# Expert loops over pairs written out; their last turn normalises and transposes tiles 0 and 1 for the stage behind them

## The reference, cut to what matters

```python
x = x + _L0_ffn_ref(_layernorm(x), gate_w, gate_b, expert_w, expert_b)   # 8 experts, the 2 best, relu
x = x + _L1_attn_ref(_layernorm(x), Wq, Wk, Wv, Wo)                      # q * cumsum(k * v), then Wo
x = x + _L1_xattn_ref(_layernorm(x), ctx_2048, ...)
x = x + _L1_ffn_ref(_layernorm(x), W1, Wg, W2, ...)                      # 1 shared and 7 routed experts, silu
x = x + _L2_attn_ref(_layernorm(x), W_qkv, W_o)                          # 16 heads, ALiBi, causal softmax
x = x + _L2_xattn_ref(_layernorm(x), ctx_2048, ...)
```

## Time and profile before

| what | us |
|---|---|
| median of 3 runs | 2199.65 |
| the runs | 2194.30 to 2200.67 |
| the profiled execution, its own time | 2198.75 |
| its span | 2197.0 |
| PE busy | 1883.8 (86%) |
| DVE busy | 1492.2 (68%) |
| ACT busy | 1083.9 (49%) |
| POOL busy | 1083.1 (49%) |
| L0f, from its first gate matmul to its last add | 434.7 to 504.0 |
| L1a, from its first matmul | 508.0 |
| L1f, from its first matmul to its last add | 564.0 to 746.8 |
| L2a, from its first matmul | 751.0 |

### The profile page before, as it was taken

One profiled execution on the slowest core, in us unless ns is written; L12 is line 12 of the kernel. 1 busy time (PEld: TensorE's weight loads), 2 busy tenths in 40 slices (PEclk: granted clock), 3 DMA queues, 4 the chain that ended last, 5 costly groups with the idle time before them and its releaser, 6 DMA issues.

```text
span 2197.0 us, 32570 instructions
## 1 busy us (share of the span) xinstructions
PE 1883.8 (86%) x11446; PEld 1386.8 (63%) x11446; DVE 1492.2 (68%) x2547; ACT 1083.9 (49%) x2348; POOL 1083.1 (49%) x791
## 2 busy tenths in 40 slices
PE   7577788798899896899999999678888789877999
PEld 6111157545789774677777777566777655545888
DVE  5688843474764484777777776489999858665543
ACT  4444422253223264666666666366666546534443
POOL 2599931120880173755555554499999800012221
PEclk9788899599899898999999999789999889998999
DMA  4111002120400010100000001000000020000000
GB/s 158 45 34 34 0 1 75 51 102 3 171 0 0 0 30 20 49 23 1 1 1 1 1 1 39 19 1 1 1 1 27 1 78 1 1 0 1 6 9 8
DMA packets 22162, 54.80 MB, mean 25 GB/s; under 512 B 8463, under 2 KB 13752, under 8 KB 19592
## 3 DMA queue, kind: packets, MB, share of 16 engines
q1 hardware_dynamic: 22024, 53.01, 7.2%
HBM read 44.61 MB, written 1.05 MB: 21 GB/s over the span
## 4 chain that ended last, share of the span: by engine, by line
PE 53%; DVE 17%; POOL 11%; issue 11%; ACT 7%; SPq 1%; DMA 0%; DVEq 0%; POOLq 0%; ACTq 0%
POOL sbuf L1308 4%; PE psum L4121 4%; DVE sbuf L2289 3%; PE psum L4182 3%; PE psum L3499 2%; PE psum L4254 2%; POOL sbuf L1316 2%; DVE psum L3084 1%; PE psum L4607 1%; POOL sbuf L1107 1%; PE psum L4628 1%; PE psum L4614 1%; PE psum L4169 1%; PE psum L4153 1%; PE psum L4125 1%
## 5 line engine op out<-in xcount | busy, mean ns | idle before, releaser
L1308 POOL TENSOR_TENSOR sbuf<-sbuf 128x1035 f32<-128x1035 f32 x128 | 248.3, 1969 | 0.9 <-ACT sbuf L1946 0.9
L4254 PE MATMUL psum<-sbuf 128*128 128x128 f32 (+1 forms) x1024 | 146.4, 295 | 58.9 <-ACT sbuf L1955 41.4
L1955 ACT ACTIVATE sbuf<-sbuf 128x1001 f32<-128x1001 f32 (+1 forms) x128 | 141.5, 1137 | 104.6 <-DVE sbuf L3092 70.6
L4254 PEld LDWEIGHTS psum<-sbuf 128*128 128x128 f32 (+1 forms) x1024 | 128.5, 155 | 80.5 <-ACT sbuf L1955 60.1
L1263 POOL TENSOR_TENSOR sbuf<-sbuf 128x512 f32<-128x512 f32 x64 | 66.7, 1042 | 187.7 <-DVE sbuf L2980 187.7
L1107 POOL TENSOR_TENSOR sbuf<-sbuf 128x1024 f32<-128x1024 f32 x64 | 149.8, 2354 | 17.0 <-DVE sbuf L2289 17.0
L2289 DVE TENSOR_TENSOR_SCAN sbuf<-psum,sbuf 128x1024 f32<-128x1024 f32 x64 | 144.7, 2278 | 12.5 <-ACT psum L1429 6.2
L3447 PE MATMUL psum<-sbuf 96*128 96x512 bf16 x256 | 83.7, 439 | 74.3 <-DVE sbuf L2289 33.0
L1879 ACT ACTIVATE sbuf<-psum,sbuf 128x128 f32<-128x128 f32 x256 | 90.6, 366 | 107.3 <-DVE sbuf L2974 107.3
L3084 DVE SCALAR_TENSOR_TENSOR psum<-sbuf,psum 128x1024 f32<-128x1024 f32 (+1 forms) x96 | 122.3, 1274 | 16.5 <-PE psum L4244 9.4
L1429 ACT ACTIVATE psum<-psum,sbuf 128x1016 f32<-128x1016 f32 x64 | 69.0, 1082 | 125.7 <-PE psum L3447 125.7
(11 more groups left out here) (895 smaller groups left out, 5143.1 us busy)
## 6 DMA issues: line engine op xcount, KB each, us to landing
sbuf<-sbuf SPq DMA_DIRECT2D x42, 128.0 KB, 2.4
sbuf<-w_p_d SPq DMA_DIRECT2D x8, 512.0 KB, 3.8
sbuf<-w_qkv_d SPq DMA_DIRECT2D x3, 768.0 KB, 4.3
sbuf<-w_e_d SPq DMA_DIRECT2D x1, 2048.0 KB, 7.8
sbuf<-w_gu_d SPq DMA_DIRECT2D x1, 2048.0 KB, 10.0
sbuf<-w_gu_d SPq DMA_DIRECT2D x2, 1024.0 KB, 7.9
sbuf<-w_dn_d SPq DMA_DIRECT2D x1, 2048.0 KB, 17.1
sbuf<-w_q_d SPq DMA_DIRECT2D x1, 2048.0 KB, 8.1
```

Of the source, the lines that this page charges most:

```text
L1308: pool.tensor_tensor(P_r[g % 7][:, :, :], rows.unsqueeze(2).to_broadcast([128, 23, 45]), cols.unsqueeze(1).to_broadcast([128, 23, 45]), AL ...
L1955: act.activation(Q_r[g % 6][:, 0:w], Q_r[g % 6][:, 0:w], ACT.Silu, scale=q8_p[n % 2][:, h:h + 1]).then_inc(silu_done, 1)
L4254: last = pe.matmul(Gps[0:m, c, :], Q_r[g % 6][:, 128 * c:128 * c + m], ident[:, :], start=h == 0 and c % 4 == 0, stop=h == 7, skip_group_c ...
```

## The change

Four things are edited.

- The loops of L0f and of L1f become Python loops, so that their four turns are written out with constants as wait values and addresses. L1a keeps its hardware loops.
- In the written-out loops the tiles prepared for the next turn are `(2 * b + 2) % 8` and `(2 * b + 3) % 8`: in the last turn tiles 0 and 1, which the first turn has finished.
- The lead-in of L1a is taken out on all engines; `unT0` and `unT1` come from the last turn of L0f.
- In L2a the statistics, factors, normalisation, transposes and copies of tiles 0 and 1 are taken out; queries, keys and values of these two tiles read `unT0` and `unT1`. The counters of later stages are lowered to match. DVE gets one more wait, ahead of its second bias add, for POOL's centring of the weights, whose scratch memory overlaps `L2a_P[1]`.

```diff
@@ POOL, ACT, DVE, PE: L0f; ACT, DVE, PE: L1f @@
-            with pe.Fori(0, 4) as b:
+            for b in range(4):
@@ DVE, L0f; the same at L2559, L2581, L2585 and in L1f at L2722, L2725, L2790, L2791 @@
-                dve.bn_stats(st0[:, 0:6], x_next[:, 2*b+0, :])
+                dve.bn_stats(st0[:, 0:6], x[:, (2 * b + 2) % 8, :])
@@ ACT, between L0f and L1a @@
-            act.sem_inc(L1a_scalar_done, 4)
-            act.wait_ge(L0f_scalar_done, 74)
-            act.wait_ge(L1a_vector_done, 6)
-            act.activation(st0[:, 8:9], st0[:, 7:8], ACT.Ln, bias=eps5[:, 0:1]).then_inc(L1a_scalar_done, 1)
...
-            act.activation(unT1[:, 0:2, :], ps1[:, 0, 0:256], ACT.Copy).then_inc(L1a_scalar_done, 1)
+            act.sem_inc(L1a_scalar_done, 9)
@@ DVE, between L0f and L1a @@
-            dve.sem_inc(L1a_vector_done, 3)
+            dve.sem_inc(L1a_vector_done, 9)
             dve.wait_ge(L0f_vector_done, 135)
-            dve.bn_stats(st0[:, 0:6], x[:, 0, :]).then_inc(L1a_vector_done, 1)
...
-            dve.tensor_scalar(u1[:, :], x[:, 1, :], st1[:, 6:7], st1[:, 9:10], ALU.subtract, ALU.mult).then_inc(L1a_vector_done, 1)
-            dve.wait_ge(L1a_matmul_done, 2)
@@ PE, between L0f and L1a @@
-            pe.wait_ge(L1a_vector_done, 8)
...
-            last.then_inc(L1a_matmul_done, 1)
+            pe.sem_inc(L1a_matmul_done, 2)
+            pe.wait_ge(L0f_scalar_done, 80)
             pe.wait_ge(L1a_w_loaded, 32)
             pe.wait_ge(L1a_scalar_done, 9)
@@ POOL, L2a @@
-            L2a_norm(0)
-            L2a_norm(1)
             for i in range(8):
@@ ACT, L2a @@
-            L2a_rstd(0, 2, 1)
-            L2a_unTc(0)
-            L2a_rstd(2, 8, 2)
             L2a_qTc(0)
+            L2a_rstd(2, 8, 1)
             L2a_vc(0)
-            L2a_unTc(1)
@@ DVE, L2a @@
                 dve.wait_ge(score_done, L2a_start['score'] + n + 1)
+                if n == 0 and a == 1:
+                    dve.wait_ge(centred_done, L2x_start['centred'] + 8)
...
             dve.wait_ge(L1f_vector_done, 253)
-            L2a_stats(0, 2)
@@ PE, L2a @@
-                pe.wait_ge(unT_done, L2a_start['unT'] + n + 1)
+                un = (unT0, unT1)[n] if n < 2 else L2a_unT
+                if n == 0:
+                    pe.wait_ge(L1f_scalar_done, 109)
+                elif n == 1:
+                    pe.wait_ge(vc_done, L2a_start['vc'] + 1)
+                else:
+                    pe.wait_ge(unT_done, L2a_start['unT'] + n - 1)
...
-            L2a_uTr(0)
             pe.wait_ge(L2a_w_loaded, 32)
             L2a_qk(0)
             L2a_value(0)
-            L2a_uTr(1)
```

More of the change, by code:

```diff
@@ L1583, in _ @@
             act.wait_ge(L0f_scalar_done, 5)
-            with act.Fori(0, 4) as b:
+            for b in range(4):
                 act.wait_ge(L0f_vector_done, 27*b + 31)
@@ L2524, in _ @@
             dve.wait_ge(L0f_scalar_done, 5)
-            with dve.Fori(0, 4) as b:
+            for b in range(4):
                 dve.wait_ge(L0f_matmul_done, 12*b + 3)
@@ L2558, in _ @@
                 dve.tensor_tensor(r0_1[:, :, :], ps1[:, 2, :].rearrange('p (e o) -> p e o', e=2), b_e0[:, 512:1024].rearrange('p (e o) -> p e o', e=2), ALU.add).then_inc(L0f_vector_done, 1)
-                dve.bn_stats(st1[:, 0:6], x_next[:, 2*b+1, :])
+                dve.bn_stats(st1[:, 0:6], x[:, (2 * b + 3) % 8, :])
                 dve.wait_ge(L0f_pool_done, 6*b + 3)
@@ L2718, in _ @@
             dve.wait_ge(L1f_scalar_done, 17)
-            with dve.Fori(0, 4) as b:
+            for b in range(4):
                 dve.wait_ge(L1f_vector_done, 51*b + 1)
                 dve.sem_inc(dve_waited, 1)
-                dve.bn_stats(st0[:, 0:6], x_next[:, 2*b+0, :]).then_inc(L1f_vector_done, 1)
+                dve.bn_stats(st0[:, 0:6], x[:, (2 * b + 2) % 8, :]).then_inc(L1f_vector_done, 1)
                 dve.wait_ge(L1f_vector_done, 51*b + 2)
                 dve.sem_inc(dve_waited, 1)
-                dve.bn_stats(st1[:, 0:6], x_next[:, 2*b+1, :]).then_inc(L1f_vector_done, 1)
+                dve.bn_stats(st1[:, 0:6], x[:, (2 * b + 3) % 8, :]).then_inc(L1f_vector_done, 1)
                 dve.wait_ge(L1f_vector_done, 51*b + 50)
@@ L4040, in L2a_value @@
                 for c in range(2):
-                    last = pe.matmul(L2a_front[:, 0:256], L2a_unT[:, c, :], w_qkv2[:, c, 512:768], start=c == 0, stop=c == 1)
+                    last = pe.matmul(L2a_front[:, 0:256], ((unT0, unT1)[n] if n < 2 else L2a_unT)[:, c, :], w_qkv2[:, c, 512:768], start=c == 0, stop=c == 1)
                 last.then_inc(v_done, 1)
```

63 lines of the change are left out of this document (17 added, 46 removed).

## The result

The changed kernel takes 2179.47 us (median of 6 runs, 2170.70 to 2181.48) where the kernel before took 2197.59 us beside it. The ratio of the means is 0.9908, 95% interval 0.9886 to 0.9931; the two medians alone give 0.9918. By these the gain is 18 to 20 us. The profiled execution took 2179.06 us. The forecast of 2184.0 against 2199.65 us is a ratio of 0.9929, so the direction was right, and the gain is some 2 to 5 us larger than the 15.7 us of the sum.

A forecast was written before the change was run, and what follows sets the result against it. PE was taken to bound the loops, and chains of small instructions on several engines the lead-ins. Terms 5.4 + 1.5 + 0.4 + 0.3 + 0.1 + 8.0 = 15.7 us, from 2199.65 to 2184.0; range 2177.5 to 2192.3.

The forecast's parts named there:

- From the first bias add on the order is the old one, moved as a whole: From L2a's first bias add on: everything later keeps its order and only starts earlier, with no further gain.
- the 0.3 us for L0f's loop: Inside L0f: writing out the loop saves 0.3 us over three turn ends, bounds 0 and 0.5.
- the 1.5 us for the clock in L1a: L1a's turn 0: PE's clock stays at its upper level, 11.09 to 9.59 us, saving 1.5 us, or 0.
- the 8.0 us for L2a: L1f's last add to L2a's first bias add: 8.0 us earlier, the middle of 7.1 and 8.9.
- L0f to L1a, 5.4 us: Border of L0f and L1a: without the lead-in L1a begins at 502.6 in place of 508.01, 5.4 us off.
- L0f's entry, 0.4 us: Entry of L0f's loop: 0.4 us saved because the loop registers go, bounds 0 and 0.4.
- my rival on turn ends: Rival (6%): jumps of ACT, DVE and POOL lie on some path; six turn ends add 2.4 us: 2181.6.
- a term only in L1f: L1f's last add: 0.1 us saved, as part of its 0.16 us delay is an address computed in registers.
- turn 1 gives it back: L1f: its entry saves 0.37 us, but turn 1, whose end POOL sets, returns it; taken as 0.
- phase rival: Rival (12%): in L1f's turns 0 and 1, DVE caught beside POOL once more, 2187.6, or not at all, 2180.2.
- A stage behind L2a that has grown: Sign that would show the forecast wrong: some stage after L2a takes longer than before; no size given.
- Code loading: Rival (3%): written-out turns load 7 blocks more; slower, 2206 us, if each costs 3.2 us.

The follow-up runs named there:

- three_turns: The changed kernel with the first three turns of L0f and L1f as hardware loops again, only the last written out; 2180.07 us, 0.9929 of the kernel before.

## Why the prediction was right in direction, and where its sum failed

The borders went as forecast, but the sum of 15.7 us was too small: the edited places gave 17.4 us and L2f another 4.3. The step that failed most is "From the first bias add on the order is the old one, moved as a whole". It put everything behind L2a's lead-in at nothing, and L2f became 4.3 us shorter. Next come two terms that were too small, the 0.3 us for L0f's loop (1.8 measured) and the 1.5 us for the clock in L1a (2.5 measured); the 8.0 us for L2a was 0.9 too large. That the time still lies inside the range is partly luck: nothing in the range was meant for L2f.

- **L0f to L1a, 5.4 us: right.** Measured 5.3. PE began 0.23 us behind the copy, not 0.43.
- **Clock in L1a's turn 0, 1.5 us: mechanism right, size off.** 2.5 us. The step that failed is taking 11.09 us for what a cold turn 0 costs; the other two profiles had 12.57 and 12.75, and 9.69 with PE kept at work.
- **L0f's entry, 0.4 us: right.** 0.45 to 0.54 us became 0.10.
- **L0f's turns, 0.3 us: too small.** Measured 1.8. "Inside L0f the turn's first matmul idles 0.16 us" was read as the cost of a turn end. The cost there is the 0.33 us between the transposes and the gates and 0.08 in the gates, the 0.4 us of my rival on turn ends. That rival holds for L0f's three alone, 1.2 us: L1f's and L1a's cost nothing, as I had it. The other 0.6 us lie inside the turns, 0.3 of it at DVE's adds that end the last one, for which I had a term only in L1f.
- **L1f's entry, "turn 1 gives it back": wrong by some 0.2 us.** The entry gave 0.3 us. Turns 0 and 1 took 94.0 us before and 94.2 after: turn 0 grew by 0.4 and turn 1 shrank by 0.2, since in turn 0 DVE's small instructions do meet POOL differently (L2710 takes 1.93 us where the same one, L2744, took 0.85). The last turn, to its last add, is 0.2 us shorter, of which the forecast had 0.1. The phase rival's price of 3.6 us didn't occur: the subtraction in turn 1 takes 3.64 us before and after.
- **L1f to L2a, 8.0 us: right within 1 us.** Measured 7.1 in the mean, 7.8 against the first profile. DVE sets the masked keys, 3.06 us behind the add (3.1 expected). I took the middle between the two clocks. The values ran at the full one in all three profiles (1.13 us), the scores at half of it in two (2.03 and 2.00 us) and partly in the third (1.75). Part of what the first profile seemed to promise was its own slow lead-in.
- **"From the first bias add on the order is the old one, moved as a whole": right to L2f, wrong there.** This is the step behind most of the missing gain, 4.3 us in L2f. 1.9 of it is one DVE instruction that no longer runs into a multiplication of POOL (43.85 against 41.97 us for the tile); for the rest the cause stays open. I had the mechanism, DVE caught beside POOL, as a rival with 12%, but looked for it only where the change is, in L1f. "A stage behind L2a that has grown" stood among my signs; one that shrank did not.
- **Code loading: didn't occur.** 8 packets more, against 7 estimated, and L1f at 182.3 us. The Trainium skill (Runtime: NRT & Kernel Launch, section Instruction fetch mechanics) calls the crossing of a block mostly hidden; the trace agrees, 182.4 us before.

## What to carry to other kernels

A lead-in between two stages costs its chain and then PE's clock behind it: preparing the first tiles in the last turn of the stage before took both away, 7.8 us at one border, and keeping PE at work in the gap gives the second part alone. What a hardware loop costs at its turn end is to be read as start to start across the jump; here it counted in L0f, where PE had no queued work at that place, and not in L1f and L1a. Where POOL and DVE both work from SBUF, a shift of 0.3 us at one instruction was worth 1.9 us, and L2f as a whole took 335.8 to 341.6 us in kernels with the same code for it. So profile both kernels more than once and compare stage by stage before crediting an edit.

## What the runs showed that I had not expected

- A delay of 0.5 us on DVE went with a stage 5.4 us longer in one kernel and 2.5 us shorter in another.
- PE idle for 1.27 us kept the full clock for the scores behind it (1.15 us), idle for 2.98 us didn't (2.03 us), though the values right behind the idle time still ran at the full clock (1.13 us) in both. In three_turns the values behind the same 2.98 us ran at half the clock (2.08 us).
- The last turn of a written-out loop, with no turn end behind it, was 0.5 us shorter as well.
- L0f's start moved by 434.0 to 440.1 us in three profiles of one kernel; the cold turn 0 of L1a by 11.09 to 12.75 us.
